# Layer four's attention: third buffer of masked scores, mask multiplication one unit ahead of the maxima, second transposes and values one step later

## The reference

```python
def attention(q, k, v, mask):
    scores = jnp.einsum('bhqd,bhkd->bhqk', q, k) / jnp.sqrt(jnp.float32(HD))
    scores = scores * mask - 10000.0 * (1.0 - mask)
    probs = jax.nn.softmax(scores, axis=-1)
    return jnp.einsum('bhqk,bhkd->bhqd', probs, v)
```

## Time and profile before

| | |
|---|---|
| median of 3 runs | 2080.44 us (2079.01 to 2082.59) |
| profiled execution: its own time | 2084.22 us |
| profiled execution: span of the trace | 2082.5 us |
| PE busy in the span | 1871.1 us (90%) |
| DVE, ACT, POOL busy | 1153.3, 971.2, 777.7 us |
| first mask multiplication to last unit's row sums | 1630.1 us to 1964.7 us of the span |

### The profile page before, as it was taken

One profiled execution on the slowest core, in us unless ns is written; L12 is line 12 of the kernel. 1 busy time (PEld: TensorE's weight loads), 2 busy tenths in 40 slices (PEclk: granted clock), 3 DMA queues, 4 the chain that ended last, 5 costly groups with the idle time before them and its releaser, 6 DMA issues.

```text
span 2082.5 us, 38527 instructions
## 1 busy us (share of the span) xinstructions
PE 1871.1 (90%) x15569; PEld 1585.3 (76%) x15569; DVE 1153.3 (55%) x2107; ACT 971.2 (47%) x2550; POOL 777.7 (37%) x819
## 2 busy tenths in 40 slices
PE   6788887798999999999999999999989788878698
PEld 5566665687888888888888888888877666656587
DVE  3444544445555555566665555556444677767543
ACT  4343344334444444444444444444444576756533
POOL 3322232222342524344253343425231576765400
PEclk9999999899999999999999999999999899999899
DMA  3000001100222323122231322222220000000000
GB/s 111 11 7 2 7 2 42 49 1 11 51 57 46 67 36 77 36 64 44 41 62 36 67 46 57 56 46 55 47 76 1 11 2 2 7 6 2 1 21 21
DMA packets 163201, 71.98 MB, mean 35 GB/s; under 512 B 136512, under 2 KB 154576, under 8 KB 163024
## 3 DMA queue, kind: packets, MB, share of 16 engines
q1 hardware_dynamic: 150672, 50.64, 12.1%
q10 hardware_dynamic: 12352, 18.88, 2.9%
HBM read 33.84 MB, written 2.10 MB: 17 GB/s over the span
## 4 chain that ended last, share of the span: by engine, by line
PE 73%; DVE 11%; ACT 8%; issue 3%; POOL 3%; DMA 1%; SPq 0%; DVEq 0%; ACTq 0%; POOLq 0%
PE ps_high L197 40%; PE ps_four L197 7%; PE ps_four L2666 5%; PE ps_four L2654 5%; PE ps_four L2459 2%; PE ps_high L2551 2%; ACT l_pt L1734 2%; POOL l_sm L1588 2%; PE ps_high L2442 2%; PE ps_four L2467 1%; DVE l_mx L2177 1%; ACT l_prob L1825 1%; DVE l_sm L2169 1%; DVE l_mx L2182 1%; ACT l_sm L1779 1%
## 5 line engine op out<-in xcount | busy, mean ns | idle before, releaser
L1835 ACT ACTIVATE l_ao<-ps_four,columns 128x512 fp32r<-128x512 f32 x128 | 88.0, 687 | 388.5 <-PE ps_four L2666 380.6
L1622 POOL TENSOR_TENSOR l_prob<-l_prob,l_mx 128x516 f32<-128x516 f32 x128 | 134.2, 1049 | 310.0 <-DVE l_mx L2210 310.0
L1825 ACT ACTIVATE l_prob<-ps_four,l_mx 128x129 f32<-128x129 f32 x512 | 181.8, 368 | 122.7 <-DVE l_mx L2203 122.6
L197 PE MATMUL ps_high<-l_hT,l_wq 128*128 128x512 f32 x768 | 211.1, 410 | 2.1 <-DVE l_hT L2092 2.1
L197 PEld LDWEIGHTS ps_high<-l_wo,l_ao 128*128 128x128 f32 x1536 | 197.7, 190 | 10.6 <-issue 0.7
L197 PE MATMUL ps_high<-l_wo,l_ao 128*128 128x256 f32 x1536 | 202.4, 281 | 0.0
L197 PE MATMUL ps_high<-l_wv,ctxT 128*128 128x512 f32 x768 | 200.7, 397 | 1.4 <-ACT l_qT L1806 1.4
L197 PE MATMUL ps_high<-ctxT,l_wk 128*128 128x512 f32 x768 | 198.2, 393 | 0.0
L1588 POOL TENSOR_TENSOR l_sm<-l_sm,l_mask 128x1024 f32<-128x1024 f32 x64 | 150.2, 2368 | 107.9 <-DVE l_sm L2169 107.8
L2216 DVE COPY l_planes<-l_prob 128x1024 uint16<-128x1024 uint16 x128 | 88.9, 694 | 149.0 <-POOL l_prob L1622 149.0
L197 PEld LDWEIGHTS ps_high<-ctxT,l_wk 128*128 128x128 f32 x768 | 144.6, 188 | 33.6 <-DVE l_V L2191 0.4
(11 more groups left out here) (295 smaller groups left out, 3830.3 us busy)
## 6 DMA issues: line engine op xcount, KB each, us to landing
l_staging<-in_L_xattn_wv ACTq DMA_DIRECT2D x8, 512.0 KB, 3.9
l_staging<-in_L_xattn_wk ACTq DMA_DIRECT2D x8, 512.0 KB, 4.2
l_staging<-in_L_xattn_wq ACTq DMA_DIRECT2D x8, 512.0 KB, 4.1
l_staging<-in_L_xattn_wo ACTq DMA_DIRECT2D x8, 512.0 KB, 3.9
ctx_tok<-in_ctx SPq DMA_DIRECT2D x8, 256.0 KB, 3.1
x_tok<-in_x SPq DMA_DIRECT2D x4, 512.0 KB, 5.4
l_raw_w<-in_L_xattn_mlp_w SPq DMA_DIRECT2D x2, 1024.0 KB, 6.8
l_planesT<-l_planes SPq DMA_TRANSPOSE x128, 3.1
```

What stands on the lines that cost most here:

```text
L197: ins = e.matmul(out, a, b, start=start and i == 0, stop=stop and i == 2, skip_group_check=not check)
L1622: e.tensor_tensor(pr[:, :, 0:S + 1], pr[:, :, 0:S + 1], mx[:, 3, :].unsqueeze(2).to_broadcast([P, GB, S + 1]), ALU.mult).then_inc(sem("poo ...
L1825: ins = e.activation(pr.t[:, b, 0:S + 1], banks[b // 2].t[:, (b % 2) * (S + 2):(b % 2) * (S + 2) + S + 1], ACT.Exp, bias=mx[:, 1, b:b + 1] ...
L1835: e.activation(ao.t[:, 0, :], bk.t, ACT.Identity, bias=self.cols(f"L2_xattn_bv{at + 1}")[:, hd:hd + 1]).then_inc(sem("act.l2_values"), 1)
```

## The change

`l3_sm` gets three buffers in place of two, and now stands behind `l3_pt` in memory. ACT's part of `l3_shift` becomes a stage of its own, `l3_shift2`, with a semaphore of its own. One turn of the loop now holds `masked(n)`, `shifted_too(n - 2)` (ACT's additions), `shifted(n - 1)` (DVE's maxima and addition), `probs(n - 2, 1)`, `scores(n + 1)`, `over_v(n - 2)` and `probs(n - 1, 0)`, with the four calls of `fill()` behind `shifted_too`, `scores`, `over_v` and the last. No instruction is added or taken out. The perceptron's buffers wait for other events than before, since other tiles lie under them.

```diff
--- before.py
+++ after.py
@@ -1209,9 +1209,12 @@
             kind, g, b = self.units[n]
             pl.slot(mx, "rowmax", n)
             pl.emit("l3_shift", n)
-            pl.free("rowmax", n, by=("act.l3_shift", n))
             if kind == "b" and b == GB - 1:
                 pl.free("mask2", g, by=("dve.l3_shift:b", n))
+
+        def shifted_too(n):
+            pl.emit("l3_shift2", n)
+            pl.free("rowmax", n, by=("act.l3_shift2", n))
 
         def probs(n, half):
             if half == 0:
@@ -1254,7 +1257,7 @@
         run(self.mlp2(3))
         last = ("pe.down3", ("l2m", G - 1), FC - 1)
         attention = ExitStack()
-        sm, pt = self.ring("l3_sm", 2, [P, 16, S], F32, attention), self.ring("l3_pt", 2, [P, 4, 4 * S], F32, attention)
+        pt, sm = self.ring("l3_pt", 2, [P, 4, 4 * S], F32, attention), self.ring("l3_sm", 3, [P, 16, S], F32, attention)
         MS = self.ring("l3_mask2_", 2, [P, 2, GB, S], F32, attention)
         for slot in (*sm.slots, *pt.slots, *MS.slots):
             slot.freed = last
@@ -1277,6 +1280,15 @@
         for n in range(N + 2):
             if n < N:
                 masked(n)
+            if n >= 2:
+                shifted_too(n - 2)
+            fill()
+            if 1 <= n <= N:
+                shifted(n - 1)
+            if n >= 2:
+                probs(n - 2, 1)
+            if n + 1 < N:
+                scores(n + 1)
             fill()
             if n >= 2:
                 while self.units[n - 2][:2] not in ready:
@@ -1287,16 +1299,9 @@
             if 1 <= n <= N:
                 probs(n - 1, 0)
             fill()
-            if 1 <= n <= N:
-                probs(n - 1, 1)
-            if n + 1 < N:
-                scores(n + 1)
-            if n < N:
-                shifted(n)
-            fill()
         attention.close()
-        probs_done, over_done = ("full", "probT", N - 1, 3), ("full", "over", "l3", N - 1)
-        self.mlp_tiles("l3e", scope, (probs_done, probs_done, over_done, ("pool.l3_masked", N - 1)))
+        over_done = [("full", "over", "l3", N - 2 + i) for i in range(2)]
+        self.mlp_tiles("l3e", scope, (*over_done, ("full", "probT", N - 1, 3), ("full", "probT", N - 1, 0)))
         weights = self.mlp_weights("l3e", ("sp.l3_mlp", 32))
         next(weights)
         run(self.mlp_input(("hs", ("l3n", 3, 0)), ("l3e", 0), h_done["l3e", 0]))
@@ -1771,13 +1776,13 @@
             q.wait_ge(*pl.event(("full", "probT", n, r)))
             e.activation(pt.t[:, r, :], bk.t, ACT.Exp, scale=float(DH) ** -0.5).then_inc(bk.slot.empty, 1)
 
-        def l3_shift(n):
+        def l3_shift2(n):
 
             sm, mx = use["sm", n].t, use["rowmax", n].t
             q.wait_ge(*pl.done("dve.l3_shift:b", n))
             for h in range(8, 16):
                 ins = e.activation(sm[:, h, :], sm[:, h, :], ACT.Identity, bias=mx[:, h:h + 1])
-            ins.then_inc(sem("act.l3_shift"), 1)
+            ins.then_inc(sem("act.l3_shift2"), 1)
 
         def ao(stage, bk, rec, ao, b, place):
 
@@ -1863,7 +1868,7 @@
             e.activation(pt.t[:].rearrange("h b t -> h (b t)"), bk.t[0:H3, :], ACT.Copy).then_inc(bk.slot.empty, 1)
 
         stages = dict(const=const, l0_qk=l0_qk, l0_project=l0_project, l0_scores=l0_scores, l1_loads=l1_loads, l1_xT=l1_xT, norm_xa=norm_xa,
-                      norm_tr=norm_tr, cols=cols, l1_probs=l1_probs, hid3=hid3, l3_keys=l3_keys, l3_queries=l3_queries, l3_probs=l3_probs, l3_shift=l3_shift, l1_ao=l1_ao, l3_ao=l3_ao,
+                      norm_tr=norm_tr, cols=cols, l1_probs=l1_probs, hid3=hid3, l3_keys=l3_keys, l3_queries=l3_queries, l3_probs=l3_probs, l3_shift2=l3_shift2, l1_ao=l1_ao, l3_ao=l3_ao,
                       l2_q=l2_q, l2_w_load=l2_w_load, m_w_load=m_w_load,
                       l2_k=l2_k, l2_scores=l2_scores, l2_values=l2_values, l2_pbT=l2_pbT,
                       phase=lambda name: self.phase_start(q, e, name))
@@ -2584,7 +2589,7 @@
 
         def l3_probs(n, r):
             sm = use["sm", n].t
-            q.wait_ge(*pl.done("dve.l3_shift:s" if r < 2 else "act.l3_shift", n))
+            q.wait_ge(*pl.done("dve.l3_shift:s" if r < 2 else "act.l3_shift2", n))
             bk = fill("probT", n, r)
             for x in range(4):
                 ins = e.transpose(bk.t[:, x * S:(x + 1) * S], sm[:, 4 * r + x, :], self.ident[:])
```

## The result

The changed kernel takes 2138.9 us (median of 4 runs, 2136.91 to 2140.86) against 2081.52 us before (2079.01 to 2083.11, 4 runs): ratio 1.0277, 95% interval 1.0259 to 1.0295. It is 57 us slower. The forecast was 2104 us and at most 2127: the side was right, the size was not. The profiled execution took 2136.91 us, with a span of 2135.2; before it was 2084.22 and 2082.5, so the two traces are 52.7 us apart.

What follows compares the result with a forecast made beforehand. It took the ACT and PE loop as the bound: 31 x 8.59 + 69.4 = 335.7 us against 314.8, 20.9 more; plus 4, less 2.4, plus 1.5 for clock, giving 2104 us (2092 to 2116; whole range 2080 to 2127).

Steps and rivals of the forecast that it cites:

- DVE's wait for POOL goes: Attention: DVE's first maxima no longer wait for POOL's mask addition, 39.9 us in 19 places.
- Subtraction and POOL's addition at nothing: Attention: DVE's subtraction always falls into POOL's addition, but delays stay below the ACT and PE loop, so costed at nothing.
- The loop of ACT and PE, 8.6 us: Attention, from one unit's values to the next: handovers between ACT and PE sum to 8.6 us, against 8.11 before.
- Side work, 69.4 us above the loop: Attention: projections, norms, copies and smaller places that PE's or ACT's idle time doesn't cover add 69.4 us.
- The clock, 1.5 us: Attention: 1.5 us added because PE's work was costed at full clock.
- the rival with the falling clock: Attention: PE's clock falls after idle pieces, half-clock share doubles to 0.36, 21 us on top, 2125 us; chance 0.17.
- The first unit, 4 us: Attention's start: first values come about 4 us later, behind 3.7 us of keys for a later unit.
- The tail, -2.4 us: Attention's end: perceptron weights may be split earlier, so PE's 2.4 us wait for DVE goes.
- The rivals with DVE: Attention: DVE sets the pace, 2050 or 2065 us, chance 0.11; DVE's side work also binds, up to 2118, chance 0.12.

Runs made afterwards that it cites:

- The two runs that open the loop: Changed kernel with old ACT/PE order a turn later, mask still ahead: 2067.2 us; changed kernel with ACT's additions before logarithm, values behind next first transposes: 2068.2 us.
- the two filled ones: Changed kernel plus twenty useless identity transposes on PE in each unit: 2120.0 us; the same only where PE has no side work there: 2114.6 us.
- the run filled where empty: Changed kernel plus twenty useless identity transposes only where PE has no side work between the halves of a unit's transposes: 2114.6 us, ratio 1.0158.
- buffers and events alone: Kernel before, its order kept, with the third buffer, new memory places and the perceptron's new events: 2077.4 us, ratio 0.9982.

## Why the prediction was right on the side and wrong on the size

- **DVE's wait for POOL goes**: right (39.9 us to 1.1).
- **Subtraction and POOL's addition at nothing**: right in the price. That the subtraction "now always falls into POOL's addition" was wrong: beside 11 of the 32 no addition of the mask ran, and only 7 took over 2 us (2.12 to 3.37). The median took 1.25 us, before 2.11, and PE waited for one only once, 0.4 us. POOL pays: its additions take up to 3.36 us, 2.60 on average, where they took at most 2.44 before. The reading of the Trainium skill's rule (SBUF — State Buffer, "SBUF: two separate sides") with DVE always losing would have lengthened the subtraction; the exclusion is there, but DVE mostly didn't lose (below).
- **The loop of ACT and PE, 8.6 us**: right at full clock (its five parts add up to 8.61; the sum went on with 8.59, which is 0.6 us in all). It measured 8.43 us where PE ran at full clock in the changed kernel, and 8.44 with the idle time filled. In the changed kernel itself plain units mostly took more: the multiplications that were to start 8.5 us apart started 9.75 apart (1668.62 and 1678.37). The two runs that open the loop take back 71 and 72 us.
- **Side work, 69.4 us above the loop**: right as a total. Taking for each of the 31 steps the shortest of the changed kernel and the two filled ones, from first to last unit's values, the sum is 334.8 us; the forecast for it was 335.7. Picking the shortest of three leans low; the best single run has 340.6.
- **The clock, 1.5 us**: this is the step that failed. I wrote "I add 1.5 for what is costed at full clock", and from first to last unit's values it took 366.1 us (367.7 between the ends of the row sums) in place of 335.7, or 337.2 with the 1.5. Filling PE's idle time where it had nothing else to do brought it back by 25.5 us, to 340.6; so 25.5 of the 30.4 missing are shown to be the clock by that run. The rest is 4.9. In that run two steps with a norm took 14.1 and 15.8 us but 12.8 and 13.4 where all places were filled, and their scores 2.09 us in place of 1.69 and 1.17, so most of the rest is the clock as well. The twelve steps without side work alone took 118.0 us in place of the 103.1 forecast, and 102.0 in the run filled where empty.
- **Why I mis-sized it**: the rival with the falling clock had the mechanism, with the idle piece and the price of a unit at half clock (3.8 us), but I took 0.36 of the time at half clock for its outer case, 21 us, and gave it 0.17. The mean clock fell only from 0.91 to 0.87, which at (1 - 0.87) / 0.5 is a share of 0.26 at half clock against 0.18. By the rival's own formula, 31 x 0.08 x 3.8, that would be 9 us; over the steps alone, from first to last unit's values, the means are 0.94 and 0.88, which makes 14. It was 25.5. No full 3.8 was paid in a plain unit (1.56 in that of 1676), but a part of it in most. But the mean is over time, idle time too, and the half clock came behind the idle piece, on the scores and values that stand in the loop: 18 of 28 batches of scores were slow, in place of 2 of 29, and 5 of 28 with the idle time filled where empty. That what PE lost before was covered by the loop of DVE and POOL is likely, but no run shows it.
- **The first unit, 4 us**: 7.9 us, of which 1 is the keys' projection at lower clock (4.65 us in place of 3.70); PE's wait for the first ACT additions, 3.43 us, I had not counted.
- **The tail, -2.4 us**: -6.9 us. The wait of 2.4 us is gone; the products behind it, which before took 1.38, 1.48 and 2.14 us, now take 0.95, 0.88 and 1.55, 1.6 us less: the clock behind an idle piece here too. The remaining 2.9 us stand in one later place, first in the kernel before, then in the changed kernel:

```profile
2051.14 5.49 PE L197 MATMUL ps_four<-l3e_mhs,l3e_w 128*128 128x512 f32 x12 [2.51 <-DVE l3e_mhs L2128]
2056.43 1.98 PE L197 MATMUL ps_high<-l3e_mhs,l3e_w 128*128 128x512 f32 x6
```

```profile
2106.72 3.02 PE L197 MATMUL ps_four<-l3e_mhs,l3e_w 128*128 128x512 f32 x12 [2.51 <-DVE l3e_mhs L2133]
2109.58 1.52 PE L197 MATMUL ps_high<-l3e_mhs,l3e_w 128*128 128x512 f32 x6
```

  The instructions are the same, those ahead of them took the same time and the idle piece is 2.51 us in both; only the granted clock differs (0.57 over 2050 to 2058 us before, 1.00 over 2105 to 2113 now). So 2.9 of the 6.9 us are no effect that I can name of the change, and may be luck of the two executions. With buffers and events alone the tail was 5.5 us shorter, of which 1.4 stand in this same place.
- **The rivals with DVE**: PE waited for DVE's multiplication in 2 places, 6.6 us, both ahead of the first unit's values, and for DVE's side work in 2, 1.4 us. So DVE doesn't bind.

The miss against its own execution (2136.9 less 2108, 28.9 us) is closed by these: 30.5 between the row sums' ends, 3.9 for the first unit, -1.2 for the earlier start, -4.5 for the tail, together 28.7.

## What to carry to other kernels

Before moving a stage later, add up the loop that it closes between two engines, as one engine's full wait list says little: here DVE's largest wait was removed for 8 to 11 us, and a loop of handovers cost 70 to 72. If such a loop leaves TensorE idle for one long piece in each round, price its instructions behind that piece at the slower durations which the trace shows for them, not by the mean clock, and take the full-clock sum as the lower bound. When an order gets faster, look again at the rate at which side work is mixed in, and give the kernel before the same new rate as a control.

## What the runs showed of the hardware

How long PE's instructions took went mostly with what PE did just before them, and work without use can be worth more than idle time: 2.35 us of useless transposes in a gap of 3.36 us took the scores behind it from 2.09 to 1.17 us and the whole kernel down by 24 us, from 2138.9 to 2114.6 (1.0277 to 1.0158 by the ratios). In the attention's last units of the changed kernel PE ran most of its instructions at the lower of its two levels, 1.2 and 2.4 GHz (values 1.93 in place of 1.08 us, granted clock 0.70 over 34 us). The idle piece alone doesn't settle it: behind pieces of 3.06 us eight transposes took 1.09 us at 1745.63 and 1.97 at 2007.48. Nor does the work ahead of it: in the tail the same products, behind the same work and the same 2.51 us, took 5.49 us in one trace and 3.02 in the other.

The second thing is how DVE and POOL come past each other. DVE's subtraction at two places of the changed kernel, and POOL's pair of additions at the same two (the second place is 54 us behind the first):

```profile
1644.37 3.37 DVE L2184 TENSOR_TENSOR l_sm<-l_sm,l_mx 128x1024 f32<-128x1024 f32 x1
...
1698.63 1.23 DVE L2184 TENSOR_TENSOR l_sm<-l_sm,l_mx 128x1024 f32<-128x1024 f32 x1
```

```profile
1644.31 5.66 POOL L1593 TENSOR_TENSOR l_sm<-l_sm,l_mask 128x1024 f32<-128x1024 f32 x2
...
1696.42 5.68 POOL L1593 TENSOR_TENSOR l_sm<-l_sm,l_mask 128x1024 f32<-128x1024 f32 x2 [3.75 <-DVE l_sm L2174]
```

The pair takes 4.67 us when nothing comes between. At 1698.63, 2.21 us behind its start, the subtraction came just before the first addition's end, took 1.23 us, and the pair took 5.68, 1 us more: it went between the two. At 1644.37, only 0.06 us behind POOL's start, it took 3.37 us, which is the rest of the first addition and its own time, and the pair was again 1 us longer. So whoever has started isn't stopped, and DVE, if it waits, comes ahead of POOL's next instruction. In all 11 places of this trace in which the subtraction started within the first addition of such a pair, the second took 3.34 to 3.36 us in place of 2.36. The earlier trace rows of the kernel before fit that as well; it is an inference from such rows, as no run took the two apart.
